# A fused two-layer attention kernel: probabilities in two arrays, weighing in 64x64 and 32-row tiles, values copied whole, two squares and two scalings on ScalarE, a new order of work

## The reference

```
# layer 0, 16 heads of 8 numbers
q, k, v  = x @ Wq + bq, ctx @ Wk + bk, ctx @ Wv + bv
s        = clip((0.5 * mask + 0.5) * (q . k) / sqrt(8), -50, 50)
y        = layernorm(x + softmax(s) @ v @ Wo + bo) * gamma + beta
# layer 1, 16 heads of 64 numbers
xn       = rms_norm(y) * w
q, k, v  = split(xn @ to_qkv_w);  q, k = rope(q), rope(k)
# each query sees 16 equal memory tokens (from the mean of ctx), 16 stored ones,
# and the tokens of its own 64-token segment up to itself
x1       = y + softmax(q . k / 8 + mask) @ v @ to_out_w
a, g     = split(rms_norm(x1) * w2 @ ff_w1 + ff_b1)
out      = x1 + (silu(g) * a) @ ff_w2 + ff_b2
```

## Time and profile before

| | us |
|---|---|
| median of 3 runs (1326.8 to 1328.15) | 1328.0 |
| the profiled execution, its own time | 1323.15 |
| its span | 1321.3 |
| granted TensorE clock over the span | 0.993 |
| TensorE busy | 1218.2 (92%) |
| VectorE busy | 1130.1 (86%) |
| GpSimd busy | 1026.5 (78%) |
| ScalarE busy | 972.7 (74%) |

### The profile page before, as it was taken

The page is one execution under the profiler, slowest core; times in us unless marked ns, Lnnn a source line. Parts: engine busy times, 40 slices in busy tenths (PEclk is TensorE's granted clock), DMA queues, the critical chain, the costliest instruction groups (busy, mean ns, idle before and its releaser), DMA issues.

```text
span 1321.3 us, 49126 instructions
## 1 busy us (share of the span) xinstructions
PE 1218.2 (92%) x18147; PEld 1077.4 (82%) x18147; DVE 1130.1 (86%) x2895; ACT 972.7 (74%) x2381; POOL 1026.5 (78%) x1419
## 2 busy tenths in 40 slices
PE   1589999999999999999999999999999999999996
PEld 1468888888888888888888888888888888888875
DVE  2578888998998998899899888989988998998982
ACT  1267777877777777787778778777777877877764
POOL 1278788788788878878887887888788788788874
PEclk9989999999999999999999999999999999999999
DMA  6323233223323322332332232233233223323310
GB/s 184 112 74 119 75 105 119 92 96 109 112 76 109 119 88 94 115 104 84 109 113 89 96 119 96 92 109 112 76 108 119 91 96 111 107 81 109 114 53 24
DMA packets 102166, 132.45 MB, mean 100 GB/s; under 512 B 12325, under 2 KB 84538, under 8 KB 102010
## 3 DMA queue, kind: packets, MB, share of 16 engines
q1 hardware_dynamic: 102138, 132.07, 30.4%
HBM read 40.31 MB, written 24.61 MB: 49 GB/s over the span
## 4 chain that ended last, share of the span: by engine, by line
PE 64%; DVE 18%; issue 8%; POOL 5%; DMA 2%; ACT 1%; DVEq 1%; SPq 0%; POOLq 0%; ACTq 0%
PE psum L965 17%; PE psum L1122 10%; PE psum L1006 9%; PE psum L997 8%; PE psum L1013 6%; DVE y L902 6%; PE psum L987 4%; POOL z L496 3%; DVE xn L815 3%; DVE less_max L795 3%; PE psum L972 2%; PE psum L1065 2%; DVE den L808 2%; PE psum L992 2%; PE psum L1045 1%
## 5 line engine op out<-in xcount | busy, mean ns | idle before, releaser
L499 POOL TENSOR_TENSOR probs<-probs,rden 128x324 f32<-128x324 f32 x256 | 183.3, 726 | 103.3 <-DVE rden L836 103.3
L965 PE MATMUL psum<-xnT,wqkv 128*128 128x128 f32 x2048 | 251.3, 276 | 0.5 <-ACT memT L580 0.3
L645 ACT ACTIVATE z<-z 77x512 f32<-77x512 f32 x256 | 157.5, 628 | 116.9 <-POOL z L496 112.2
L965 PEld LDWEIGHTS psum<-xnT,wqkv 128*128 128x128 f32 x2048 | 240.1, 193 | 1.0 <-ACT memT L580 0.5
L786 DVE TENSOR_TENSOR ra<-psum,rope 128x512 f32<-128x512 f32 x256 | 175.4, 685 | 19.9 <-PE psum L965 19.9
L786 DVE TENSOR_TENSOR rb<-psum,rope 128x512 f32<-128x512 f32 x256 | 173.9, 679 | 0.0
L791 DVE TENSOR_TENSOR z<-psum,wT 77x512 f32<-77x512 f32 x256 | 167.7, 675 | 6.9 <-PE psum L972 6.9
L496 POOL TENSOR_SCALAR z<-z 77x512 f32<-77x512 f32 x256 | 159.4, 630 | 14.5 <-DVE z L791 14.5
L530 POOL TENSOR_SCALAR tanh_gate<-tanh_gate 128x384 f32<-128x384 f32 x64 | 96.4, 1506 | 95.4 <-ACT half_gate L639 95.4
L580 ACT ACTIVATE probsT<-psum 81x512 f32<-81x512 f32 x256 | 145.6, 595 | 29.9 <-PE psum L997 29.8
L490 POOL TENSOR_TENSOR qT<-ra,rs 128x512 f32<-128x512 f32 x128 | 162.8, 1272 | 3.5 <-DMA rs<-rb 3.5
(11 more groups left out here) (130 smaller groups left out, 2743.0 us busy)
## 6 DMA issues: line engine op xcount, KB each, us to landing
rs<-rb SPq DMA_DIRECT2D x256, 256.0 KB, 2.4
qk_dram<-qk_parts SPq DMA_DIRECT2D x64, 307.5 KB, 4.4
qk_stack<-qk_dram SPq DMA_DIRECT2D x256, 76.9 KB
seq_in<-in SPq DMA_DIRECT2D x64, 166.5 KB
out<-out_sb SPq DMA_DIRECT2D x64, 64.0 KB, 1.9
maskT<-in SPq DMA_DIRECT2D x64, 38.5 KB
vall<-memv_dram SPq DMA_DIRECT2D x128, 4.0 KB
ctx_all<-in SPq DMA_DIRECT2D x5, 320.0 KB, 5.7
```

The costliest lines, as they stand in the source:

```text
L499: return nc.gpsimd.tensor_tensor(probs[:, 4 * t:4 * t + 4, :], probs[:, 4 * t:4 * t + 4, :], rden1[:, 4 * t:4 * t + 4].unsqueeze(2).broadc ...
L645: return nc.scalar.activation(zt, zt, ACT.Exp, scale=float(HD0) ** -0.5)
L965: last = mm(at(name)[:, S * n:S * (n + 1)], wqkv[:, lo + 128 * n:lo + 128 * (n + 1)], xnT[:], start=n == 0)
```

## The change

- The probabilities leave `normalised` in two arrays: 64 columns of the segment in `probs_near`, and the 17 others in `probs_pre`, where each head has 32 columns. Two heads of `probs_near` or four of `probs_pre` are transposed at once, 128 columns wide: three transposes a group for four.
- The values are copied whole, 128 partitions at a time, into `vals`. Where a head's keys lie in the other half of the partitions, its values come from `vals_far`, which SP fills with two transfers a turn. The 17 other rows lie in `vals_pre` in bands of 32 partitions; SP refreshes the memory row with one transfer for two.
- `weigh` is one step for all heads: 32 matmuls of 64 rows by 64 columns of weights with 64 moving columns, then 16 of 17 rows by 64 with 128, into four banks `o0` to `o3`.
- Groups 0 and 1 no longer have the largest score subtracted by TensorE. Their exponential is one instruction a head, with the value as its bias.
- The two mean squares and the two scalings to `xn` and `hn` go from VectorE to ScalarE; the epsilon is a column of the operand. Intermediates of the layer norm stay in PSUM. The rotation table of q holds the factor 1/8. The tanh step on GpSimd is multiply and add in place of add and add.
- Banks, leads and the lists of all engines are new. The projections are at lead 4, both halves of the scores at lead 3. The order of TensorE is now: `weigh_cross(2, 3)`, `turned2`, `gate`, `pv`, `weigh`, `scores(0)`, `c0T`, `lin`, `wo`, `out`, `v1`, `scores(1)`, the cross scores, `v0`, `less_maxima(3)`, `(2)`, `xnT`, `down`, `turned1`, `k0`, `q0`, `hnT`, `turned0`, `q1`, `k1`, `turned3`, `qkv`, `weigh_cross(0, 1)`.
- The order of VectorE is: `rotary("k1")`, the rests of q and k, division by the sums, `largest(0)`, `(1)`, `through_gate`, the sum with `wo` and its statistics, the row sums of group 0, `x1`, centring, the row sums of group 1, `y`, two reciprocals, `largest(3)`, `(2)`, `masked(0)`, `(1)`, `(2)`, the row sums of group 3, `masked(3)`, a reciprocal, `rotary("k0")`, `("q0")`, the row sums of group 2, `out_sb`, a reciprocal, `rotary("q1")`.
- The order of SP is: memory row, exchange of the second half (waits for `rotary("k1")`), the write of `qk_parts`, its four reads, the output, `vals_far`, the inputs, exchange of the first half.

```diff
+                slots, scale = slice(4 * t, 4 * t + 4), rden1[:, 4 * t:4 * t + 4].unsqueeze(2)
+                nc.gpsimd.tensor_tensor(probs_near[:, slots, :], probs[:, slots, 0:SEG], scale.broadcast_to([S, 4, SEG]), ALU.mult)
+                return nc.gpsimd.tensor_tensor(probs_pre[:, slots, 0:PRE], probs[:, slots, SEG:KEYS], scale.broadcast_to([S, 4, PRE]), ALU.mult)
...
+                if t in SHIFTED_BY_PE:
+                    return nc.scalar.activation(probs[:, 4 * t:4 * t + 4, :], heads(f"scores{t}"), ACT.Exp)
+                for n in range(4):
+                    last = nc.scalar.activation(probs[:, 4 * t + n, :], at(f"scores{t}")[:, KEYS * n:KEYS * (n + 1)], ACT.Exp,
+                                                bias=less_max[:, 4 * t + n:4 * t + n + 1])
...
+                return copy(probsT[:, t, :], at(f"turned{t}")[:, 0:3 * S])
...
+                return copy(vals[:, BANK * t:BANK * (t + 1)], at(f"v{t}"))
+
+            def keep_heads(n):
+                return copy(oT[:].rearrange("p (f n) i -> p f n i", f=2)[:, :, n, :], at(f"o{n}")[:, 0:2 * S].rearrange("p (f i) -> p f i", f=2))
+
+            def mean_square(scratch, rows, total):
+                return nc.scalar.activation(scratch, rows, ACT.Square, scale=float(D) ** -0.5, accum_out=total)
...
+            def weigh():
+                for f in range(2):
+                    for j in range(2):
+                        for s in range(NSEG):
+                            for h in range(2):
+                                for p in range(2):
+                                    n, dims, keys = 2 * j + p, slice(DH * h, DH * (h + 1)), slice(SEG * p, SEG * (p + 1))
+                                    head = 2 * (4 * f + n) + h
+                                    near = vals[keys, DH * head:DH * (head + 1)] if p == s else vals_far[keys, 2 * f + j, dims]
+                                    mm(at(f"o{n}")[dims, S * f + SEG * s:S * f + SEG * (s + 1)], near,
+                                       probsT[keys, 2 * f + h, S * j + SEG * s:S * j + SEG * (s + 1)], start=f == 0 and s == 0)
+                for f in range(2):
+                    for n in range(4):
                         for h in range(2):
...
+                            keys = slice(BAND * n, BAND * n + PRE)
+                            last = mm(at(f"o{n}")[DH * h:DH * (h + 1), S * f:S * (f + 1)], vals_pre[keys, 2 * f + h, :],
+                                      probsT[keys, 2 * f + h, 2 * S:3 * S], start=False)
                 return last
```

In SP's list, the part between the memory row and the reads:

```diff
+                if seq[3] is not None:
+                    sp.wait_ge(k1_rotated, done[4])
                     passed(sp, sp_passed)
-                    for s in range(NSEG):
-                        sp.dma_start(vall[s][SEG:SEG + 1, :], memv_dram[bass.ds(seq[2], 1), :]).then_inc(memv_in, 16)
+                    for odd in range(2):
+                        sp.dma_start(rs[odd::2, half(1)], rb[1 - odd::2, half(1)]).then_inc(swapped1_in, 16)
                 if seq[5] is not None:
-                    sp.wait_ge(q_rest_ready, done[6])
+                    sp.wait_ge(k_rest_ready, done[6])
```

More of the change, by code:

```diff
@@ L28 @@
 PRE = 1 + NPM
+BAND = 32
 VROW = HD0 + 1
@@ new lines, in build @@
+            ("turned2", 2, 2, (probsT2_ready,)),
+            ("gate", 0, 1, (gate_ready,)),
+            ("pv", 1, 4, (c0_ready,)),
+            ("scores1", 5, 3, (probs1_exp,)),
+            ("o0", 6, 2, (oT0_ready,)),
+            ("o1", 4, 2, (oT1_ready,)),
+            ("o2", 2, 2, (oT2_ready,)),
+            ("o3", 7, 2, (oT3_ready,)),
+            ("c0T", 0, 4, (c0T_ready,)),
+            ("lin", 1, 1, (sT_ready,)),
+            ("wo", 0, 4, (y_ready,)),
+            ("out", 2, 2, (x1_ready,)),
@@ L463, in body @@
                         context_loads(0, 1)
+                if seq[4] is not None:
+                    sp.wait_ge(q0_rotated, done[5])
+                    passed(sp, sp_passed)
+                    for odd in range(2):
+                        sp.dma_start(rs[odd::2, half(0)], rb[1 - odd::2, half(0)]).then_inc(swapped0_in, 16)
             pipeline(sp, body)
@@ L516, in body @@
[L516 to L526, removed]
@@ L538, in body @@
                     nc.gpsimd.tensor_copy(kall[:, :, :, SEG:SEG + 1], mk)
+                if seq[1] is not None:
+                    wait(pool, out_ready, done[1])
+                    nc.gpsimd.tensor_tensor(x1b[:], x1[:], b2_rep[:], ALU.add)
+                if seq[3] is not None:
                     pool.wait_ge(swapped0_in, done[4] * 32)
@@ new lines, in body @@
+                if seq[5] is not None:
+                    copy(wT[:], maskT[:], scale=0.5, bias=0.5).then_inc(wT_ready, 1)
+                if seq[3] is not None:
+                    act.wait_ge(v1_filled, done[4])
+                    values(1).then_inc(vals1_ready, 1)
+                if seq[4] is not None:
+                    act.wait_ge(y_ready, done[5])
+                    mean_square(ysq[:], y_eps[:], st0[:, 4:5]).then_inc(ms0_ready, 1)
+                    act.wait_ge(rms0_ready, done[5])
+                    copy(xn[:], y[:], scale=st0[:, 6:7]).then_inc(xn_ready, 1)
@@ new lines, in body @@
+                if seq[3] is not None:
+                    act.wait_ge(shifted2_filled, done[4])
+                    exp_self(2).then_inc(probs2_exp, 1)
+                    values(0).then_inc(vals0_ready, 1)
+                if seq[4] is not None:
+                    if first(seq[4]):
+                        pooled_tokens()
+                    if first(seq[4]):
+                        act.wait_ge(early_in, EARLY_IN)
+                    act.wait_ge(xnT_ready, done[5])
+                    copy(xnT_hi[:], xnT[:]).then_inc(xnT_hi_ready, 1)
+                    if first(seq[4]):
+                        value_weight_parts()
@@ L712, in body @@
-                if seq[3] is not None:
-                    if first(seq[3]):
+                    act.wait_ge(hnT_filled, done[3])
+                    copy(hnT[:], at("hnT")[:, 0:S], scale=cols[:, FW:FW + 1]).then_inc(hnT_ready, 1)
+                if seq[4] is not None:
+                    if first(seq[4]):
                         act.wait_ge(consts_cast, 1)
@@ L992, in less_maxima @@
                 return mm(at(f"scores{t}")[:, 0:4 * KEYS].rearrange("i (n k) -> i n k", n=4), ident_b[:],
-                          less_max[:, 4 * t:4 * t + 4].unsqueeze(2).broadcast_to([S, 4, KEYS]), start=False)
+                          less_max_b[:, 4 * t:4 * t + 4].unsqueeze(2).broadcast_to([S, 4, KEYS]), start=False)
             def turn(t):
-                for n in range(4):
-                    last = nc.tensor.transpose(at(f"turned{t}")[0:KEYS, S * n:S * (n + 1)], probs[:, 4 * t + n, :], ident[:])
@@ L998, in turn @@
-                return last
-            def weigh(f):
-                for n in range(4):
-                    for s in range(NSEG):
+                p = at(f"turned{t}")
+                for j in range(2):
+                    pair = probs_near[:, 4 * t + 2 * j:4 * t + 2 * j + 2, :].rearrange("i n k -> i (n k)")
+                    nc.tensor.transpose(p[:, S * j:S * (j + 1)], pair, ident[:])
+                return nc.tensor.transpose(p[:, 2 * S:3 * S], probs_pre[:, 4 * t:4 * t + 4, :].rearrange("i n k -> i (n k)"), ident[:])
```

662 lines of the change are left out of this document (315 added, 347 removed).

## The result

| | before | after |
|---|---|---|
| median, 9 runs each | 1327.73 us (1325.1 to 1330.61) | 1318.14 us (1315.27 to 1326.41) |
| span of the profiled execution | 1321.3 | 1313.5 |
| cross scores: the fifth / the last of 64 start at | 108.42 / 1252.50 | 127.20 / 1253.43 |
| one turn, mean from the fifth to the last | 19.39 | 19.09 |
| drain, from there to the end | 68.8 | 60.1 |

The ratio is 0.9937 (95% 0.992 to 0.9954): 0.6% faster, where 1.3% was forecast. The table splits the 7.8 us between the two profiled executions: the 59 turns from the fifth to the last of the 64 cross scores give 0.30 x 59 = 17.8, the drain (the last turns, as the pipeline runs empty) 8.7, and the fill (the first turns, up to the fifth sequence) takes 18.8 back.

A forecast was written before the change was run, and what follows sets the result against it. The loop through cross scores, rotations, exchange, write and reads was taken to set the turn at 19.1 us for 19.35: 16 us over 64 turns, 1 off fill and drain, hence 1311 us from 1328.0; range 1262 to 1350.

The forecast's parts named there:

- The deciding loop: Cross scores, DVE's masks and rotations, SP's exchange, write, reads, back to cross scores: 19.1 us a turn.
- The fill: First and last turns, some 80 us with the drain: -1 us, within +-6.
- The write: Write of `qk_parts` in the deciding loop: 4.48 and 0.1, plus 0.1 to 0.2 for the exchange's traffic.
- Weighing: `weigh` on PE: 1.46 for 32 near matmuls, 1.0 for 16 band matmuls, together 2.46 us for 2.01.
- The second loop, through ACT: From `xs` over late inputs, `qkv`, weighing, ACT's copies, exponentials and masks to the scores: 18.5 us against 19.1.
- The slower rival: ACT's chain behind `weigh` delays the scores: 20.45 us a turn, 1398 us, likely part 1336 to 1368; chance 31%.
- DVE and `y`: DVE falls from 17.49 to about 14.5 us a turn; `y`, one operand in PSUM, takes some 0.3 for 1.28.
- The tanh step: On POOL, 1.51 us: may fall by up to 1.0 or not at all.
- PE as the bound (15%): Rival: PE's 17.85 us and 0.4 of waits set the turn, 18.25, giving 1257 us; chance 15%.

The follow-up runs named there:

- The work added in the loop and off it: Changed kernel with two unused row sums more on VectorE: between the rotations 1399.46 us, ahead of `largest(0)` 1301.09 us; changed kernel on the next occasion 1300.84.
- the repaired kernel: Changed kernel with the context sums after both rests and the memory values stored a turn earlier: 1292.26 us, 8.6 below the changed kernel beside it.
- writing first: Changed kernel with SP issuing the write of `qk_parts` ahead of the exchange of the second half: 1310.02 us, turn 18.91.
- cutting both: Changed kernel with inputs ahead of `vals_far`, write ahead of exchange, and rests not waiting for the copy to v0: 1291.12 us, beside 1300.84.
- 0.75 more: Changed kernel with `project("v1")` done twice, about 0.75 us more TensorE work a turn: 1301.04 us, turn 18.84.

## Why the prediction was right and wrong

- *The deciding loop: right.* 19.1 us was worked out and 19.09 measured. The terms agree too: cross scores to the last rotation 9.3 for 9.2, SP 1.4, the write 4.73 for 4.7 to 4.8 with the exchange's traffic, reads 3.6 for 3.8. PE idles ahead of the cross scores, `qk_stack` is named, and the write follows the exchange on SP. The work added in the loop and off it shows it to be the bound, and not only where the wait appears. One thing was luck: I had VectorE's masks as the way from the cross scores to the rotations, and PE's steps up to `k0` were 0.15 us longer.
- *The fill: this step failed.* "They lose a few tanh and SBUF stalls and keep their waits for transfers: -1, within +-6" measured 18.8 - 8.7 = +10.1. It took back more than half of what the turns gave. With it, 1311 + 11 = 1322 would have stood against 1318. I took fill and drain over as a lump and never walked the first turns through the diff, where two causes can be read: the sums moved in between the rests, and the store of the memory values, unmoved in SP's list, came to stand shortly ahead of its user. Putting both back gave 8.6 us, the stretch at the lower clock included. The other half is no cause that I tested. In the repaired kernel the first cross scores start at 18.3, as before, and the third at 76.8 for 69.4, so 7.4 of the 8.5 us left arise in between. There the third sequence's write leaves at 67.8, behind the steps for the memory tokens and the weighing of the cross values, and stands in line with its reads and the cross scores; before it left at 53.3, well ahead of them.
- *The write: a single number for one that moves.* 4.7 to 4.8 us with hand-over and the exchange's traffic was right on the first occasion, 4.73, so the miss there is the fill's alone. On the other two it was 4.50 and 4.42, and since it now lies in the loop, 0.31 us a turn is 18 us in all. That 1311 lies between the occasions (1318, 1301, 1296) is luck: on the later two a shorter write outweighs the longer fill. The row it came from is one transfer early in the run.
- *Weighing: wrong, without effect.* 2.46 was taken, 1.88 to 5.8 allowed, 1.71 measured: near 1.09 / 32 = 0.034 each, under my lower end of 0.036, which scaled with the columns, and the bands 0.62 / 16 = 0.039, under 0.046. The Trainium skill says in TensorEngine Tiling (Array Packing), Key Properties, that a change of tiling mode drains TensorE. If so, the drain is small here: between the near part and the bands, starts go from 903.93 to 904.08.
- *The second loop, through ACT.* I put it at 18.5, with slack 0.6; the trace has scores(1) end at about 909.9 and the cross scores start at 911.25, 1.3 us of slack, since weighing is short. The slower rival needed +0.9 and got less than nothing. The loop that did stand next, over the inputs and POOL to `y`, I had only in pieces. It is why writing first gained nothing by itself, and the third loop is why cutting both gave 10 us and not 47.
- *DVE and `y`: right.* 14.76 us for the 14.5 expected, and `y` takes 0.35 for 1.28 once an operand lies in PSUM, although POOL's `xb` runs beside it (909.57 to 910.02). The Trainium skill's VectorE: DVE Perf Modes, Two Vector instructions with no wait between them, has the second SBUF read interface shared with GpSimd, and the trace agrees; no run puts the operand back. The tanh step fell by the upper end of its bound, 1.51 to 0.51. ACT is busy 15.5, a little under my 15.9 to 16.5.
- *PE as the bound (15%): wrong.* Its own work fell to about 17.1 us (18.1 less 0.7 for transposes and largest scores, less 0.3 for weighing), and 0.75 more changed nothing.

## What to carry to other kernels

When every engine has slack and the time still stands, look for the loop: follow the chain of waits over one whole turn, and test it by putting the same work once into the loop and once off it. An order of work can hide a DRAM round trip or put it in line; in line, its spread becomes the kernel's. A new order also reorders the fill, which is to be walked step by step, and cutting the longest loop gains only as much as the next one leaves.

## What the runs showed of the hardware

- The same kernel ran at 1318, 1301 and 1296 us on three occasions, with the kernel before at 1327.4 to 1327.7 each time; the write of 307.5 KB to DRAM took 4.73, 4.50 and 4.42 us to the first read's issue, while an exchange within SBUF took 2.4 each time.
- 64x64 tiles of fp32 with 64 moving columns went at 0.034 us a matmul, four 32-row bands of 17 rows by two column halves with 128 moving columns at 0.039.
- PE's steps took up to twice as long where the granted clock lay at its lower level, 1.2 GHz: `down` 1.28 us for 0.67, weighing and scores ahead of `c0T` in the fill 4.4 for 2.4.
- A POOL tensor_scalar of 128x384 took 1.51 us as add, add and 0.51 as multiply, add.
- ScalarE's exponential of 81 columns with a bias, eight in a row, took 1.88 us: 0.21 each from start to start, though one record is 0.365. Its square with a sum carries a separate read of the accumulator of 0.19.
